# Last tile's gate logits from unnormalised rows, a seven-way threshold search, other counts of spare products, an earlier gather and a halved last group

## The chip, the cores and the metric

The kernel runs on one core of one Trainium2 chip. The metric is the device time in microseconds (us) of one execution. Three runs of the kernel before gave a median of 479.52 us (479.47 to 480.42). A core has five engines that run their own instruction streams and wait for one another on semaphores: TensorE (PE, matmuls), VectorE (DVE), ScalarE (ACT), GpSimd (POOL) and SyncE (SP, which here only issues DMAs).

## What is computed

The inputs are `x` (1250 rows of 512 features), 20000 edges, and weights. The reference, cut to what matters:

```python
xn = layernorm(x)
x = x + gnn(xn, edges, W1, b1, W2, b2) + mix(xn, Wq, Wk, Wv, mW1, mW2)   # two graph layers; linear attention
y = layernorm(x)                                  # 1250 rows, the "final" normalised rows
# routing, one group of 1250 tokens, 8 experts, m = 1250 // 8 = 156 places for each expert
logits = y @ gate_weight                          # 1250 x 8
t = log(clip(logits, 1e-6))
for _ in range(8):                                # Sinkhorn
    t = t - logsumexp(t, over tokens)
    t = t - logsumexp(t, over experts)
gates = exp(t)
vals, idx = top_k(gates.T, m)                     # the 156 best tokens of each expert
out = y[idx[e]] @ experts[e] * vals[e]            # for each expert e
x = x + scatter(out)                              # where two experts took a token, the later one stands
```

## The kernel before

The 1250 rows are ten tiles of 125. The kernel computes x's normalisation and K (to about 45 us), the attention terms, the adjacency counts and the first graph layer, then the second layer's aggregation tile by tile (from about 322 us), and then the routing and the experts.

At the start, SP issues the loads in an order written out by hand: x part 0, two chunks of Wk, x part 1, the other two chunks of Wk, the rest of x (L475 to L482). PE runs 12 spare products on a filled tile, transposes tile 0 (`turn_x(0)`, L714), runs 8 more spare products (`warm(WARMER)`, L715) and then the K products, in which the transposes of the next tiles stand at a fixed place (L718 to L722).

The stage around the change begins in the loop at L957. For tile i, `collect(i)` sums the aggregation in PSUM (L930 to L950). DVE (loop at L1727) adds it to X, takes mean and variance, waits for ACT's reciprocal root (L1265), makes the final factor in three small steps (`inverse_root`, L1306 to L1308) and writes the normalised row Y (L1737). PE transposes Y (`turn_y`, L913), ACT copies the transposes (`copy_yt`, L1250), and PE multiplies by the gate weights (`logits`, L920). For the last tiles PE runs 8 spare products (`keep_clock`, L952) while it waits; they write a PSUM bank that nobody reads. SP stores X and Y of each tile to a scratch tensor in HBM (`store_x`, `store_y`) and then loads the other experts.

Next come eight Sinkhorn rounds on P8 (125 x 10 x 8): DVE sums over the tiles, PE sums over the partitions by a product with ones (L974), DVE takes the reciprocal and scales, then normalises over the experts (L1751 to L1757). Each round has 4 spare products on PE behind the sum. Then ten rounds of a search for each expert's threshold, three bits of the number's pattern at a time (L1759 to L1772). DVE compares P8 with 8 candidates for each expert in two halves of five tiles (MASK), PE counts by ten products with ones (L983) and runs 4 spare products, and DVE keeps the largest candidate that at least 156 tokens reach (MET, kth) and makes the next candidates (THR).

From the threshold DVE and PE compute ties, ranks and each token's slot (L1783 to L1817), and one product gives the token number of each of the 128 slots in ten columns: eight experts, and two groups that hold 32 places for each of four experts beyond their 128 (`slots`, L1000 to L1005). DVE turns it into indices (L1827 to L1829), after which GpSimd gathers rows of scratch (`gather`, L620). The gate values go through a like product (`gates`, L1008), with 7 spare products before and 11 behind it. Each column is then transposed (`turn_slot`), copied (L1277, L1281), multiplied by its expert (`expert`, L1021) or, for the two groups, by four experts in strips of 32 (`rests`, L1035), weighed and added by DVE (`weigh`, L1848) and scattered to the output by GpSimd (L630). The order of the columns is one group, the eight experts, the other group.

The order on every engine is written out in the program. PSUM banks are given out by `psum_plan` (L71), which names who must have read a bank before it is opened again. `link` (L1288) makes DVE wait for its own last instruction; without it the next one may start before the last has written.

## Time and profile before

| what | value |
|---|---|
| median of three runs | 479.52 us |
| the profiled execution | 480.92 us |
| its span | 479.2 us |
| mean granted clock of PE | 0.983 |
| busy: PE, PE weight loads, DVE, ACT, POOL | 96%, 77%, 68%, 30%, 12% |
| the chain that ended last | PE 88%, DVE 7%, DMA 2% |

The profile is one execution, and its times count from the span's start. The chain of waits is followed back from the last instruction, at each step to what released it. The granted clock is given as a share of PE's full 2.4 GHz. Ends of matmuls are modelled, so a matmul's own duration is longer than its distance to the next; distances between starts are the better measure. The stages stand at these times: K products to 45 us, graph and attention products to 322 us, the aggregation tiles to 377.9 us, Sinkhorn from 383.9 us, the search from 400.8 us, ranks and slots from 425.2 us, gather and experts from 433 us to the end.

### The profile page before, as it was taken

How to read it: one execution, taken by the hardware profiler on the slowest of the kernel's cores; microseconds unless marked ns; L12 is line 12 of the kernel's file. 1: busy time of each engine (PE TensorE's matmuls, PEld its weight loads, DVE VectorE, ACT ScalarE, POOL GpSimd, SP SyncE). 2: the span in 40 equal slices, each digit the busy share in tenths (PEclk: the TensorE clock that was granted, in tenths of full speed). 3: DMA queues.
4: the chain of work that ended last, by engine and by line, in shares of the span. 5: the costliest groups of instructions: out<-in, count | busy, mean ns of one | idle time of the engine just before them, and what ended most of it. 6: DMA issues, size and time to landing. Idle time of an engine off the chain costs nothing.

```text
span 479.2 us, 6735 instructions
## 1 busy us (share of the span) xinstructions
PE 458.1 (96%) x2420; PEld 368.8 (77%) x2420; DVE 323.8 (68%) x1099; ACT 141.8 (30%) x244; POOL 57.7 (12%) x80
## 2 busy tenths in 40 slices
PE   7999999999999999999999999999999978877995
PEld 3787788888888888887789998778888855654782
DVE  6995698998998988896740112444446566676971
ACT  4676463333233232351231011221221135000120
POOL 4088100000000000000003000010000000005542
PEclk9999999999999999999999999999999987899998
DMA  7902004720000000003000000008444494005791
GB/s 221 271 1 88 2 0 122 182 89 23 0 2 0 2 0 1 2 1 124 1 1 3 1 0 3 0 0 288 149 130 130 131 359 166 1 1 198 262 346 76
DMA packets 20299, 40.43 MB, mean 84 GB/s; under 512 B 2408, under 2 KB 2738, under 8 KB 20259
## 3 DMA queue, kind: packets, MB, share of 16 engines
q1 hardware_dynamic: 18019, 32.53, 21.8%
q0 software_dynamic: 2240, 7.39, 4.2%
q8 instruction: 23, 0.38, 0.3%
q14 instruction: 17, 0.14, 0.1%
HBM read 30.09 MB, written 10.30 MB: 84 GB/s over the span
## 4 chain that ended last, share of the span: by engine, by line
PE 88%; DVE 7%; DMA 2%; issue 1%; SPq 0%; POOLq 0%; ACT 0%; DVEq 0%
PE ps L673 47%; PE ps L938 9%; PE ps L890 9%; PE ps L781 6%; PE ps L660 5%; PE ps L983 2%; PE ps L955 2%; PE ps L1044 2%; PE ps L923 1%; PE ps L1018 1%; DMA YX<-scratch,idx 1%; PE ps L813 1%; DMA X<-in_x 1%; PE ps L707 1%; PE ps L917 1%
## 5 line engine op out<-in xcount | busy, mean ns | idle before, releaser
L1554 DVE TENSOR_SCALAR RING_D<-places,PLACES 125x170 bf16<-125x170 f16 (+1 forms) x239 | 61.7, 258 | 0.0
L1555 DVE TENSOR_SCALAR RING_S<-iota,HOME 125x128 bf16<-125x128 f16 x239 | 58.5, 245 | 0.0
L890 PE MATMUL ps<-AT,H1H 125*128 125x416 f32 (+1 forms) x108 | 38.0, 352 | 0.0
L890 PE MATMUL ps<-AT,H1L 125*128 125x416 f32 (+1 forms) x108 | 38.0, 351 | 0.0
L938 PE MATMUL ps<-H2H,AT 125*125 125x512 f32 x90 | 36.2, 402 | 0.0
L938 PE MATMUL ps<-H2L,AT 125*125 125x512 f32 x90 | 35.5, 394 | 0.0
L955 PE MATMUL ps<-WE0H 128*128 128x512 f32 x109 | 35.3, 457 | 0.0
L1622 DVE TENSOR_TENSOR ps<-ps,bias 125x512 f32<-125x512 f32 x20 | 14.0, 699 | 27.9 <-PE ps L673 27.9
L1701 DVE SCALAR_TENSOR_TENSOR ZL<-ps,ZH 128x416 fp32r<-128x416 f32 (+1 forms) x12 | 6.3, 584 | 38.7 <-ACT ZH L1245 38.7
L660 PEld LDWEIGHTS ps<-RING_D,RING_S 125*125 125x125 bf16 x239 | 25.7, 136 | 7.9
L660 PE MATMUL ps<-RING_D,RING_S 125*125 125x170 bf16 (+1 forms) x239 | 28.6, 236 | 0.0
L565 POOL TENSOR_TENSOR G2L<-RAW_G,G2H 128x512 fp32r<-128x512 f32 x4 | 5.0, 1298 | 191.7 <-ACT G2H L1062 191.7
L621 POOL DMA_INDIRECT YX<-scratch,idx x10 | 11.9, 1188 | 112.3 <-DVE idx L1829 109.5
L955 PEld LDWEIGHTS ps<-WE0H 128*128 128x128 f32 x109 | 21.7, 218 | 3.3
L1195 ACT ACTIVATE AT<-ps 125x510 fp32r<-125x510 f32 (+1 forms) x25 | 14.8, 591 | 30.6 <-PE ps L660 30.6
L1730 DVE SCALAR_TENSOR_TENSOR X<-ps,X 125x512 f32<-125x512 f32 x10 | 6.9, 692 | 22.1 <-PE ps L950 22.1
L890 PEld LDWEIGHTS ps<-AT,H1H 125*128 125x128 f32 x108 | 20.3, 188 | 0.3
L890 PEld LDWEIGHTS ps<-AT,H1L 125*128 125x128 f32 x108 | 20.3, 188 | 0.2
L938 PEld LDWEIGHTS ps<-H2H,AT 125*125 125x125 f32 x90 | 16.7, 186 | 3.9
L938 PEld LDWEIGHTS ps<-H2L,AT 125*125 125x125 f32 x90 | 16.7, 186 | 3.8
L673 PE MATMUL ps<-CPH,QTH 128*125 128x512 f32 x40 | 17.4, 435 | 0.0
L673 PE MATMUL ps<-WQH,XTH 128*125 128x512 f32 x40 | 17.4, 435 | 0.0
(366 smaller groups left out, 1177.6 us busy)
## 6 DMA issues: line engine op xcount, KB each, us to landing
RAW_E<-in_experts SPq DMA_DIRECT2D x8, 1024.0 KB, 10.1
RAW_AGAIN<-in_experts SPq DMA_DIRECT2D x3, 1024.0 KB, 11.1
X<-in_x SPq DMA_DIRECT2D x1, 2240.0 KB
out_x<-X SPq DMA_DIRECT2D x10, 224.0 KB
scratch<-X SPq DMA_DIRECT2D x10, 224.0 KB
scratch<-Y SPq DMA_DIRECT2D x10, 224.0 KB
RAW_K<-in_WkT SPq DMA_DIRECT2D x4, 256.0 KB, 4.6
RAW<-in_mW2T SPq DMA_DIRECT2D x1, 1024.0 KB, 12.3
```

What stands on the lines that cost most here:

```text
L621: nc.gpsimd.indirect_dma_start(out=YX[0:SLOT, j % RING].rearrange("p a f -> p (a f)"), out_offset=None, in_=scratch, in_offset=bass.Indire ...
L660: pe.matmul(PS[4 + g % 2][0:TT, o:o + width(b)], hot_s(v)[:, 0:TT], hot_d(v, width(b)), start=(s == 0), stop=(s == VISITS[b] - 1), skip_gr ...
L673: mm = pe.matmul(ps, stationary[a](c), moving[b](c), start=(first and n == 0), stop=(last and n == len(pairs) - 1))
L781: mm = pe.matmul(ps[:], x[0:TT, i, f], e[0:TT, i % 4, :], start=(i == 0 and n == 0), stop=(i == NT - 1 and n == 2))
L890: pe.matmul(place(f), h[0:TT, k, 128 * f:128 * (f + 1)], AT[0:TT, k, c0:c1], start=(k == 0 and n == 0), stop=False)
L938: pe.matmul(ps, AT[0:TT, k, t], h[0:TT, k, :], start=(k == 0 and n == 0), stop=False)
L955: pe.matmul(PS[bank][:], WEH[0][:, 0, 0:128], WEH[0][:, 0, :], start=True, stop=True)
L983: mm = pe.matmul(ps[0:TT, 0:NE * WAYS], ones16[0:TT, 0:TT], MASK[0:TT, i].rearrange("p e c -> p (e c)"), start=(i == 0), stop=(i == NT - 1))
L1195: nc.scalar.activation(AT[0:TT, :, lo:hi], counts_of(g), ACT.Copy).then_inc(done["adj_hi"], 1)
L1554: V.tensor_scalar(hot_d(v, width(b)), places[0:ET, 0:width(b)], PLACES[0:ET, c:c + 1], None, ALU.is_equal)
L1555: V.tensor_scalar(hot_s(v), iota[0:ET, :], HOME[0:ET, c:c + 1], None, ALU.is_equal).then_inc(done["marked"], 1)
L1622: V.tensor_tensor(ps, ps, bias[layer - 1][0:TT, :], ALU.add).then_inc(done["h1_biased" if layer == 1 else "h2_biased"], 1)
```

## The change

1. The last tile's logits are computed from X, not from Y: `logits = rstd * (X @ gw) - mean * rstd * colsum(gw)`. PE transposes X(9) as soon as it is final (`turn_last`). The column sums of the gate weights come from a second load (`gw1`, behind x part 1) and four products with ones at the start, in the place of four of the eight spare products there. ACT copies the transposes of tiles 8 and 9 before it takes the last tile's root. Y(9) is written inside the first Sinkhorn round. The 8 spare products before the last tiles become 3 behind the last logits. The tables of the search and the two splits of expert 1 move to earlier tiles.
2. The search compares with seven candidates (the eighth, the threshold so far, is always reached and is copied into MET) and its masks are cut at tiles 6 and 4.
3. Six spare products follow each Sinkhorn sum (eight the last) where there were four.
4. DVE makes the indices ahead of the gate terms, and GpSimd's gathers wait for the first of the three index steps (`from_ready`). Two membership steps change places and one `link` goes.
5. The groups' transposed rows are copied in halves, and the last group's products and weighing run in two halves of its columns, the second in its own bank (`foot`).

The diff, cut to its core (declarations, semaphores' names and PSUM plan entries are left out):

```diff
 WAYS = 2 ** RADIX
+LANES = WAYS - 1
 HALF = NT // 2
+MASKED = [(0, 6), (6, NT)]
 TP = NE_T // 2
...
     load_x(1)
+    sp.dma_start(gw1[:], rows(gate_w[0])).then_inc(loads["gate1"], 16)
     load_wk(2)
...
     pool.wait_ge(done["st_scratch"], 2 * 16 * len(CUTS) * NT)
-    pool.wait_ge(done["idx_ready"], 1)
+    pool.wait_ge(done["from_ready"], 1)
...
     turn_x(0)
-    warm(WARMER)
+    pe.wait_ge(loads["gate1"], 16)
+    ps = opens("gsums")
+    for c in range(C):
+        mm = pe.matmul(ps[0:TT, 0:NE], ones[:, 0:TT], gw1[:, c, :], start=(c == 0), stop=(c == C - 1))
+    closes("gsums", mm)
+    warm(WARMER - 4)
     for i in range(NT):
...
+    def turn_last():
+        i = NT - 1
+        pe.wait_ge(done["x_final"], NT)
+        opens(f"yt{i}")
+        for c in range(C):
+            mm = pe.transpose(view(f"yt{i}")[:, c, 0:TT], X[0:TT, i, 128 * c:128 * (c + 1)], ident[0:TT, 0:TT])
+        closes(f"yt{i}", mm)
...
         pe.wait_ge(done["yt_ready"], i + 1)
+        ps = opens("last")[0:TT, 0:NE] if i == NT - 1 else PS[plan["logits"][0]][0:TT, NE * i:NE * (i + 1)]
         for c in range(C):
-            mm = pe.matmul(PS[plan["logits"][0]][0:TT, NE * i:NE * (i + 1)], YT[:, i % 2, c, 0:TT], gw[:, c, :],
-                           start=(c == 0), stop=(c == C - 1))
+            mm = pe.matmul(ps, YT[:, i % 2, c, 0:TT], gw[:, c, :], start=(c == 0), stop=(c == C - 1))
         if i == NT - 1:
+            closes("last", mm)
+        elif i == NT - 2:
             closes("logits", mm)
...
-    for i in range(NT + 2):
-        if i < NT:
-            collect(i)
-        if i == NT:
-            pe.wait_ge(done["x_final"], NT - 2)
-            pe.wait_ge(done["exp_hi"], 1)
-            keep_clock(8, plan[f"o{NT - 3}"][0])
-        if 1 <= i <= NT:
+    for i in range(NT):
+        collect(i)
+        if i:
             turn_y(i - 1)
...
             logits(i - 2)
+    turn_last()
+    logits(NT - 2)
+    logits(NT - 1)
+    pe.wait_ge(done["exp_hi"], 1)
+    keep_clock(3, plan[f"o{NT - 3}"][0])
...
                                      start=True, stop=True))
-        keep_clock(4, plan["order"][0])
+        keep_clock(6 if r + 1 < SINKHORN else 8, plan["order"][0])
     pe.wait_ge(done["rconsts"], 1)
...
         ps = opens(f"rad{r}")
-        for h in range(2):
+        for h, (lo, hi) in enumerate(MASKED):
             pe.wait_ge(done["ind_ready"], 2 * r + h + 1)
-            for i in range(HALF * h, HALF * (h + 1)):
-                mm = pe.matmul(ps[0:TT, 0:NE * WAYS], ones16[0:TT, 0:TT], MASK[0:TT, i].rearrange("p e c -> p (e c)"),
+            for i in range(lo, hi):
+                mm = pe.matmul(ps[0:TT, 0:NE * LANES], ones16[0:TT, 0:TT], MASK[0:TT, i].rearrange("p e c -> p (e c)"),
                                start=(i == 0), stop=(i == NT - 1))
...
-        pe.wait_ge(done["ftr_ready"], NC - COLUMNS[j])
-        ps = opens(f"fo{j}")
-        for c in range(C):
-            if c == 2 and between is not None:
-                between()
-            for q in range(4):
-                p = slice(REST * q, REST * (q + 1))
-                mm = pe.matmul(ps[p, :], FTR[:, c, p], raw[q][:, c, :], start=(c == 0), stop=(c == C - 1), skip_group_check=True)
-                if c == C - 1:
-                    mm.then_inc(done["rest_ready"], 1)
-        closes(f"fo{j}", pe.nop())
+        pe.wait_ge(done["ftr_half"], NC - COLUMNS[j])
+        parts = [(f"fo{j}", 0, D)] if between is not None else [(f"fo{j}", 0, D // 2), ("foot", D // 2, D)]
+        for name, lo, hi in parts:
+            ps = opens(name)
+            for c in range(C):
+                if c == 2:
+                    pe.wait_ge(done["ftr_ready"], NC - COLUMNS[j])
+                    if between is not None:
+                        between()
+                for q in range(4):
+                    p = slice(REST * q, REST * (q + 1))
+                    mm = pe.matmul(ps[p, 0:hi - lo], FTR[:, c, p], raw[q][:, c, lo:hi], start=(c == 0), stop=(c == C - 1),
+                                   skip_group_check=True)
+                    if c == C - 1:
+                        mm.then_inc(done["rest_ready"], 1)
+            closes(name, pe.nop())
...
             split_expert(i - 4)
+        if i == NT - 1:
+            copy_yt(i - 1)
+            copy_yt(i)
         if i < NT:
...
                                  bias=eps[0:TT, 0:1]).then_inc(done["sqrt2_ready"], 1)
-        if i:
+        if 0 < i < NT - 1:
             copy_yt(i - 1)
...
                 act.wait_ge(done["rest_ready"], 4)
-            copy(FTR[:], view(f"ft{j}")).then_inc(done["ftr_ready"], 1)
+            copy(FTR[:, 0:2], view(f"ft{j}")[:, 0:2]).then_inc(done["ftr_half"], 1)
+            copy(FTR[:, 2:C], view(f"ft{j}")[:, 2:C]).then_inc(done["ftr_ready"], 1)
         else:
...
     split_lo("wk", 3)
+    reads(dve, "gsums")
+    V.tensor_copy(gate_sum[t], ps_of("gsums")[t, 0:NE]).then_inc(done["gsum_ready"], 1)
     moments(2, statistics(2))
...
+    def normal_row(i):
+        V.tensor_scalar(Y[0:TT, i, :], X[0:TT, i, :], mv[0:TT, i, 0:1], rstd[0:TT, 2, i:i + 1],
+                        ALU.subtract, ALU.mult).then_inc(done["y_ready"], 1)
+    def radix_tables():
+        after("rconsts", 1)
+        for r, s in enumerate(SHIFTS):
+            V.tensor_scalar(ctab[:, r, :], lane[:], WAYS - 1, s, ALU.bitwise_and, ALU.logical_shift_left)
+        V.tensor_scalar(THR[:], lane[:].unsqueeze(1).broadcast_to([128, NE, LANES]), WAYS - 1, SHIFTS[0], ALU.bitwise_and,
+                        ALU.logical_shift_left)
+        V.memset(MET[:, :, 0:1], 0.0)
...
         after("inv2_ready", i + 1)
-        V.tensor_scalar(Y[0:TT, i, :], X[0:TT, i, :], mv[0:TT, i, 0:1], rstd[0:TT, 2, i:i + 1],
-                        ALU.subtract, ALU.mult).then_inc(done["y_ready"], 1)
-        if i in (6, 7):
-            expert_left(1, i - 6)
-    after("rconsts", 1)
-    for r, s in enumerate(SHIFTS):
-        V.tensor_scalar(ctab[:, r, :], lane[:], WAYS - 1, s, ALU.bitwise_and, ALU.logical_shift_left)
-    V.tensor_scalar(THR[:], lane[:].unsqueeze(1).broadcast_to([128, NE, WAYS]), WAYS - 1, SHIFTS[0], ALU.bitwise_and,
-                    ALU.logical_shift_left)
+        if i < NT - 1:
+            normal_row(i)
+        if i in (5, 6):
+            expert_left(1, i - 5)
+        if i == 7:
+            radix_tables()
+    i = NT - 1
+    link(V.scalar_tensor_tensor(away[t, i:i + 1], mv[t, i, 0:1], -1.0, rstd[t, 2, i:i + 1], ALU.mult, ALU.mult))
+    link(V.tensor_scalar(last8[t, 0, :], gate_sum[t], away[t, i:i + 1], None, ALU.mult))
     reads(dve, "logits")
-    link(V.tensor_scalar(P8[t], ps_of("logits")[t, 0:NT * NE].rearrange("p (i e) -> p i e", e=NE), CLIP_EPS, None, ALU.max))
+    V.tensor_scalar(P8[t, 0:i, :], ps_of("logits")[t, 0:i * NE].rearrange("p (i e) -> p i e", e=NE), CLIP_EPS, None, ALU.max)
+    reads(dve, "last")
+    link(V.scalar_tensor_tensor(last8[t, 1, :], ps_of("last")[t, 0:NE], rstd[t, 2, i:i + 1], last8[t, 0, :], ALU.mult, ALU.add))
+    link(V.tensor_scalar(P8[t, i, :], last8[t, 1, :], CLIP_EPS, None, ALU.max))
     for r in range(SINKHORN):
...
+        if r == 0:
+            normal_row(NT - 1)
         reads(dve, f"sink{r}")
...
     for r in range(len(SHIFTS)):
-        for h in range(2):
-            w = slice(HALF * h, HALF * (h + 1))
-            V.tensor_tensor(MASK[t, w], P8[t, w].unsqueeze(3).broadcast_to([TT, HALF, NE, WAYS]),
-                            THR[t].bitcast(F32).unsqueeze(1).broadcast_to([TT, HALF, NE, WAYS]),
-                            ALU.is_ge).then_inc(done["ind_ready"], 1)
+        for lo, hi in MASKED:
+            shape = [TT, hi - lo, NE, LANES]
+            V.tensor_tensor(MASK[t, lo:hi], P8[t, lo:hi].unsqueeze(3).broadcast_to(shape),
+                            THR[t].bitcast(F32).unsqueeze(1).broadcast_to(shape), ALU.is_ge).then_inc(done["ind_ready"], 1)
+        if r:
+            V.tensor_copy(MET[t, :, 0], kth[t])
         reads(dve, f"rad{r}")
-        V.scalar_tensor_tensor(MET[t], ps_of(f"rad{r}")[t, 0:NE * WAYS].rearrange("p (e c) -> p e c", c=WAYS), float(TOPK),
-                               THR[t].bitcast(F32), ALU.is_ge, ALU.mult).then_inc(done["count_read"], 1)
+        V.scalar_tensor_tensor(MET[t, :, 1:WAYS], ps_of(f"rad{r}")[t, 0:NE * LANES].rearrange("p (e c) -> p e c", c=LANES),
+                               float(TOPK), THR[t].bitcast(F32), ALU.is_ge, ALU.mult).then_inc(done["count_read"], 1)
         after("count_read", r + 1)
...
         if r + 1 < len(SHIFTS):
-            link(V.tensor_tensor(THR[t], kth[t].bitcast(I32).unsqueeze(2).broadcast_to([TT, NE, WAYS]),
-                                 ctab[t, r + 1, :].unsqueeze(1).broadcast_to([TT, NE, WAYS]), ALU.bitwise_or))
+            link(V.tensor_tensor(THR[t], kth[t].bitcast(I32).unsqueeze(2).broadcast_to([TT, NE, LANES]),
+                                 ctab[t, r + 1, :].unsqueeze(1).broadcast_to([TT, NE, LANES]), ALU.bitwise_or))
...
     running(ahead, mine).then_inc(done["order_in"], 1)
-    V.tensor_scalar(member[t, 0, :], top[t], GROUPS * 2 + 0.5, None, ALU.is_lt)
+    V.tensor_scalar(member[t, 1, :], top[t], GROUPS * 2 + 0.5, None, ALU.is_gt)
     V.tensor_scalar(shift32[t, 0, :], top[t], float(REST), -float(REST + SLOT), ALU.mult, ALU.add)
-    link(V.tensor_scalar(member[t, 1, :], top[t], GROUPS * 2 + 0.5, None, ALU.is_gt))
+    link(V.tensor_scalar(member[t, 0, :], top[t], GROUPS * 2 + 0.5, None, ALU.is_lt))
+    V.scalar_tensor_tensor(shift32[t, 1, :], member[t, 1, :], -4.0 * REST, shift32[t, 0, :], ALU.mult, ALU.add)
...
-    link(V.scalar_tensor_tensor(shift32[t, 1, :], member[t, 1, :], -4.0 * REST, shift32[t, 0, :], ALU.mult, ALU.add))
     reads(dve, "order")
...
+    reads(dve, "slots")
+    u = slice(0, SLOT)
+    ps = ps_of("slots")[u, 0:NC]
+    V.tensor_scalar(idx[u, 0, :], ps, -1.0, 0.0, ALU.add, ALU.max).then_inc(done["from_ready"], 1)
+    link(V.tensor_scalar(tokv[u, 2, :], ps, 0.0, 8192.0, ALU.is_equal, ALU.mult))
+    V.scalar_tensor_tensor(idx[u, 1, :], ps, -1.0, tokv[u, 2, :], ALU.add, ALU.add).then_inc(done["idx_ready"], 1)
     V.tensor_scalar(side[t, 0, :], rank[t, 0, :], full_slots, None, ALU.is_lt)
...
     link(V.tensor_reduce(gres[t, 0, :], w8[t].rearrange("p e i -> p i e"), AX, ALU.add))
-    reads(dve, "slots")
-    u = slice(0, SLOT)
-    ps = ps_of("slots")[u, 0:NC]
-    V.tensor_scalar(idx[u, 0, :], ps, -1.0, 0.0, ALU.add, ALU.max)
-    link(V.tensor_scalar(tokv[u, 2, :], ps, 0.0, 8192.0, ALU.is_equal, ALU.mult))
-    V.scalar_tensor_tensor(idx[u, 1, :], ps, -1.0, tokv[u, 2, :], ALU.add, ALU.add).then_inc(done["idx_ready"], 1)
...
             dve.wait_ge(scattered[j % 4], 16 * (j // 4))
-        V.scalar_tensor_tensor(FO[u, j % 4, :], ps_of(f"fo{j}")[u, :], tokv[u, 1, column(j)], YX[u, j % RING, 1, :],
-                               ALU.mult, ALU.add).then_inc(done["fo_ready"], 1)
+        for name, lo, hi in ([(f"fo{j}", 0, D)] if j + 1 < NC else [(f"fo{j}", 0, D // 2), ("foot", D // 2, D)]):
+            if lo:
+                reads(dve, name)
+                after("rest_ready", 12)
+            ins = V.scalar_tensor_tensor(FO[u, j % 4, lo:hi], ps_of(name)[u, 0:hi - lo], tokv[u, 1, column(j)],
+                                         YX[u, j % RING, 1, lo:hi], ALU.mult, ALU.add)
+        ins.then_inc(done["fo_ready"], 1)
```

## Rows read from the trace of the kernel before

**Rows 1.** The page: granted clock in 40 slices; the chain by engine.

```profile
PEclk9999999999999999999999999999999987899998
...
PE 88%; DVE 7%; DMA 2%; issue 1%; SPq 0%; POOLq 0%; ACT 0%; DVEq 0%
```

**Rows 2.** Waits of PE, 30 to 60 us: us in total, times, longest.

```profile
PE ps L726 <- DVE diag L1492: 0.3, 1, 0.3
```

**Rows 3.** Stretches: busy time of each engine, then PEclk, DMA share, GB/s.

```profile
384.00:386.00 2.00, 1.72 (x6) 1.38 (x6) 1.36 (x6) 0.00 (x0) 0.00 (x0) 0.63 0.90 294
...
402.00:404.00 2.00, 2.00 (x10) 1.53 (x9) 1.27 (x5) 1.60 (x1) 0.00 (x0) 0.50 0.00 0
```

**Rows 4.** Timeline of the last tile: start us, us, engine, line, operation, idle before.

```profile
377.47 0.39 PE L950 MATMUL ps<-H2L,AT 125*125 125x512 f32 x1
...
379.57 0.29 ACT L1265 ACTIVATE rstd<-mv,eps 125x1 f32<-125x1 f32 x1 [5.15 <-DVE mv L1733]
...
379.77 0.57 ACT L1062 ACTIVATE YT<-ps 128x500 f32<-128x500 f32 x1
...
380.65 0.55 DVE L1737 TENSOR_SCALAR Y<-X,mv,rstd 125x512 f32<-125x512 f32 x1
...
381.73 1.88 PE L923 MATMUL ps<-gw,YT 128*125 128x8 f32 x16
...
383.93 0.29 DVE L1751 TENSOR_REDUCE s<-P 125x8 f32<-125x80 f32 x1
```

**Rows 5.** Timeline of the start, 6.8 to 12 us.

```profile
6.86 1.85 PE L696 MATMUL ps<-HOT_D 128*128 128x500 bf16 x8
...
7.36 0.69 DVE L1322 BATCH_NORM_STATS2 stat<-X 125x6 f32<-125x512 f32 x1 [0.50 <-DMA X<-in_x]
...
9.49 1.40 DVE L1340 TENSOR_SCALAR XF<-X,mv,rstd 125x512 f32<-125x512 f32 x1
...
9.78 0.63 ACT L1062 ACTIVATE WKH<-RAW_K 128x512 fp32r<-128x512 f32 x1 [0.53 <-DMA RAW_K<-in_WkT]
...
10.95 0.65 PE L707 MATMUL ps<-ident,XF 125*128 125x125 f32 x4 [0.86 <-DVE XF L1340]
```

**Rows 6.** DMA issues of the whole span: KB, us from issue to landing.

```profile
gw<-in_gate SPq DMA_DIRECT2D x1, 16.0 KB, 2.0
```

**Rows 7.** Timeline of one Sinkhorn round.

```profile
390.98 1.18 PE L955 MATMUL ps<-WE0H 128*128 128x512 f32 x4
...
392.82 0.38 PE L974 MATMUL ps<-s,ones 125*125 125x8 f32 x2 [0.66 <-DVE s L1751]
```

**Rows 8.** The chain in order of time, search: start us, us, what.

```profile
402.58 1.87 PE ps L955 x4
...
405.46 1.87 PE ps L955 x4
...
414.26 0.50 DVE MASK L1762
...
416.50 0.50 DVE MASK L1762
```

**Rows 9.** Timeline behind the search, 431 to 440 us.

```profile
431.72 0.30 PE L1004 MATMUL ps<-PLACE,RS 125*128 125x10 f16 x5 [0.36 <-DVE RS L1817]
...
432.70 0.17 DVE L1829 SCALAR_TENSOR_TENSOR idx<-ps,tokv 128x10 int32<-128x10 f32 x1
...
435.04 2.79 PE L955 MATMUL ps<-WE0H 128*128 128x512 f32 x11
...
438.34 0.66 PE L1018 MATMUL ps<-ident,YX 128*128 128x128 f32 x4 [0.52 <-DMA YX<-scratch,idx]
...
439.03 0.60 ACT L1062 ACTIVATE FTR<-ps 128x512 f32<-128x512 f32 x1 [34.72 <-PE ps L1018]
```

**Rows 10.** The chain in order of time, last group.

```profile
470.40 3.69 PE ps L1044 x32
...
474.17 0.76 DVE FO L1856
```

24 lines of the change are left out of this document (15 added, 9 removed).

## The prediction

> **What bounds the kernel now.** I read the page first, then the chain of waits, then the stretches by clock. The page gives 88% of the chain to TensorE (PE) and 7% to VectorE (DVE) [rows 1]. From 12 us to 377.8 us the waits show PE waiting for another engine once, for 0.3 us [rows 2], so whatever delays it early is carried to the end and nothing there takes it back. From 377.8 us on the work is serial: DVE and PE hand small results to each other, and each instruction's latency counts. The second row of the page's picture shows something more: the granted clock is below 9 tenths in three slices, all in this serial part [rows 1]. In the table of stretches the clock goes to its lower level, 1.2 of 2.4 GHz (0.50), after 384.5 us, and again from 401.6 to 411.8 us [rows 3]. The first follows a stretch in which PE had only transposes and gate products of 8 columns (381.25 to 383.6 us) and waited [rows 4]; the second follows the last Sinkhorn round with its four spare products and the wait for the first mask.
>
> **The start.** A second load of the gate weights (512 pieces of 32 bytes) goes into SyncE's queue behind the second x part and ahead of the last two chunks of Wk and all further x. Four column-sum products (8 instructions, 0.87 us at the rate of the gate products, 16 in 1.88 us [rows 4], of which about 1.74 to the next start) take the place of four spare products of 8 that took 1.85 us [rows 5]: 0.87 for 0.9, nothing. But PE now waits for the load. On an idle queue the same load landed in 2.0 us [rows 6]. Here it stands behind x, whose landing DVE awaited until 7.36 us [rows 5], so I put it at about 7.9 to 8.4 us, against the 7.0 us at which PE is free. That moves the first K product from 8.9 to 9.8 or 10.2 us. PE stood idle for 0.86 us ahead of the transposes of the second tile [rows 5], and that idle time takes 0.86 of it. The other path is the Wk chunk: ScalarE (ACT) already waited 0.53 us for the last one [rows 5], so each tenth that the load takes from the DMA engines arrives there, less some 0.4 us of slack before DVE takes it up at 10.81 us, and one copy of the sums (0.17) joins DVE's queue. Ends: nothing, if the load lands with x, to +1.6, if PE's wait brings the clock down as it did at 384.5 us, so that four spare and four K products run at half rate (8 times 0.21). I take +0.7, between, nearest to the path by Wk. A GpSimd subtraction ran beside DVE's normalising of tile 1, which took 1.40 us [rows 5], where the same step on the last Y took 0.55 [rows 4]. A later Wk chunk may part the two, and then 0.85 us of the loss comes back. The Trainium skill says so too (SBUF — State Buffer, on the port pair that VectorE and GpSimd share, an exclusive lock: whoever comes second blocks); by that rule alone the start costs nothing, and the total would be 0.7 us lower.
>
> **The last tile.** Before, the way from the last aggregation product to the first column sum of the Sinkhorn part is 377.88 to 383.93 us: residual, statistics, root, three small steps, Y, transposes, copy, products, clip [rows 4]. After, the transposes of X run beside the statistics and the products beside the root, so that DVE's chain is last. It is longer than it looks, since ACT must finish the copy of tile 9's transposes before the root: transposes from 378.95 to about 379.55 us, copy 0.57 [rows 4], root at 380.18 instead of 379.57, so 0.61 late. Then the three steps as before (0.78 to their signal: 381.26), and in place of Y five operations: away and last8 at 0.25 each with their waits, the clip of nine tiles at 0.15 since nothing waits for it, the joining and the last clip at 0.25 each. The column sum starts at 382.41, 1.52 us earlier. PE's products end near 381.3 us and are not late. Y of the last tile (0.55) moves beside the first column-sum product; that reply took 0.46, so 0.1 is not covered. Sum: -1.4. The store of Y is 2 us later on SyncE, and the loads of experts 2 to 7 behind it too; the last of these was split at 404.3 us and is needed after 450 us. The tables of the search move to tile 7, into DVE idle time of over 1.2 us per tile. Were neither covered, 2 us and 1 us would be at stake.
>
> **Sinkhorn with six spare products.** A round is 2.08 us at full clock. PE's share is 0.38 plus four products at 0.21, and it then idles 0.66 us by the modelled ends [rows 7]; two more take 0.43, so they are hidden at full clock, and so are the eight of the last round. At half clock four took 1.87 [rows 8], 0.47 each: six and the sum product take 3.2 us, 1.1 us more than a round. The kernel before lost 0.2 to its half-clock stretch here. Ahead of this part the change takes eight spare products away and puts three back, with gate products and a wait around them, so that PE has even less to do from 377.8 us on and I expect the clock to fall once here too. One round and a bit at 3.2 costs 1.1; against the 0.2 of before, +0.9. Ends: -0.2 (no fall) and +2 (two rounds).
>
> **The search.** At half clock its round was 2.88 us (402.58 to 405.46), at full clock 2.24 (414.26 to 416.50) [rows 8], and ten rounds took from 400.82 to 425.18 us, where ten full ones less the last threshold update take 22.1: 2.2 us lost. PE set the pace in them: its ten products and four spare ones left no gap. Eight spare products at the end of Sinkhorn, where four had preceded the fall, should keep the clock: -2.2 (0 if they don't). Seven lanes for eight and the cut at 6 and 4 tiles save 80 of 640 elements, 0.08 us, on the second mask only; the first grows by 16 elements, 0.02 us, and the ten products follow it without a gap, bound by their weight loads (0.80 us for ten). The added copy of kth runs during DVE's wait of 0.57. So the lanes come to 0, at most 0.1 a round either way.
>
> **Behind the search.** Reordering the membership steps takes one wait off the path: -0.1. The gather waits for the first index only, and the indices now stand ahead of the gate terms. The product for the slots ends at 432.02 us, the first index would start at 432.06 and be ready at 432.25, where 432.87 was the third's end [rows 9]: the first gather is 0.63 earlier, and lands at 437.7 for 438.34. But the gate terms are pushed back by 0.5 (three index steps now stand ahead), and PE's eleven spare products with them: issued from 435.04, they end by 437.4 [rows 9], now 437.9. PE so takes up the gathered rows at 437.9: -0.45, not -0.63. Copying the transposed rows in halves lets the group start after half of 0.60 [rows 9]: -0.25. Sum: -0.7. The gate terms' half microsecond also delays DVE's splits, which had 2.84 us free before the first expert. **The last group** in column halves: before, 3.69 us of products, then 0.76 on DVE [rows 10]. Half the columns take DVE about 0.48, so -0.3 if the products take no longer. There are 64 for 32, each half as long; four that go to different strips start together every 0.43 us, and in the search weight load and product pairs were 56 ns apart, which for 4 pairs is 0.22, as long as 256 columns last. Ends: -0.35 and +0.3. The Trainium skill (TensorE: Matmul & The Clock Gate, "Wait — 56ns, not 53.3ns?") has about 62 ns per MATMUL of sequencer time in one of the two ways of decoding. By it, 64 products would take 4.0 us and the step would win nothing; the pairs at 56 ns of this trace speak for the other way, not strongly.
>
> **The sum.** +0.7 - 1.4 + 0.9 - 2.2 - 0.1 - 0.7 - 0.3 = -3.1. The profiled execution took 480.92 us, 1.7 more than its span, so the sum gives 477.8. The median of the three runs is 1.40 below that execution. If the whole of it is overhead of profiling, the median after is 476.4. If the runs behind the median had no half-clock stretch in the search, 2.2 of the gain is not theirs and they come to 478.6. I take 477.5.
>
> **Rivals.** (1) The clock stays up from the last tile to the end, as it did from 412 us on [rows 1]; then the Sinkhorn term is -0.2 and the start costs 0 to 0.7: 475.9 to 476.6, say 476.3. Against it: fewer spare products exactly where it fell. (2) The gain is paid back at half clock: the wait for the gate load brings the clock down at the start (+1.6) and Sinkhorn loses two rounds (+2): 479.5, within 0.2%. For it: the start's spare work is halved and stands behind a DMA. (3) The spare products don't do what they are for, and the search runs at half clock as before: 477.5 + 2.2 = 479.7. This is weakened by the fact that four per round kept the clock from 412 us on. (4) Slower: six spare products are too many at half clock. Once down, PE is the pace of Sinkhorn, 3.2 for 2.08 us; if the fall is not taken back after one round, each further round adds 1.1, and all eight add 8, to about 485. It decides from four rounds on (477.5 + 3.3 = 480.8). Against it: the clock came back at 387.9 us after a stretch in which PE was busy throughout at half rate, and six products make it busier.
>
> **Chances.** Forecast 0.52, rival (1) 0.22, (2) 0.12, (3) 0.10, (4) 0.04. A difference under 0.2% (0.96 us) cannot be told from none here. Faster by over that is 478.56 or less: the forecast and (1), and a quarter of (2) and (3), 0.78 together. Within it 0.18, slower 0.04. The range reaches from below rival (1) to the edge of (2): 475.4 to 479.5.
>
> **What would show it.** First column sum at about 1.5 us after the three small steps, and 4.5 us, not 6.05, behind the last product; root about 0.6 late behind the copy. The search's rounds all 2.24 us with a granted clock of 1.00; Sinkhorn rounds of 3.2 us under 0.50. Transposes of the first gathered rows right behind the last of eleven spare products, with no wait for the DMA. DVE's last operation near 0.48 us. The first K product at about 10 us. I am wrong if the search still has rounds of 2.88 us, or if the first K product starts after 11 us.

## The result, and the profile after

The changed kernel takes 477.36 us in the median of five runs (476.29 to 477.96); in the same rounds the kernel before took 479.55 us (479.47 to 480.88). The ratio on record is 0.9928, with a 95% interval from 0.9908 to 0.9947: faster by 0.5 to 0.9%. It isn't the quotient of these two medians, which is 0.9954; it fits the 480.5 to 480.8 us that the kernel before took beside the experiments. A second set of runs of the unedited changed kernel (experiment 10) gave 476.88 against 480.75 us, a ratio of 0.9925. The forecast was 477.5 us.

The two profiled executions are 477.36 us (span 475.3) and 480.92 us (span 479.2). This is the page of after, its granted clock in 40 slices and its chain by engine, to be held against [rows 1]:

```profile
PEclk9999999999999999999999999999999979999999
...
PE 89%; DVE 7%; issue 1%; DMA 1%; SPq 0%; POOLq 0%; ACT 0%; DVEq 0%
```

Four slices were below 9 before, three in the serial part and the last one, which lies behind the last product; one is now. The table cuts both executions at the same DVE instructions. X(9) is the start of the last residual, "sum" the first column sum of Sinkhorn, "mask" the first mask of the search, RS the first of the two instructions that write RS.

| stretch, us | before | after | forecast | measured |
|---|---|---|---|---|
| start of the span to X(9) | 377.90 | 378.13 | +0.7 | +0.2 |
| X(9) to sum | 6.03 | 4.29 | -1.5 | -1.7 |
| sum to mask (Sinkhorn) | 16.89 | 18.16 | +1.0 | +1.3 |
| mask to the ties (search) | 24.36 | 21.61 | -2.2 | -2.75 |
| ties to RS (ranks) | 4.94 | 4.82 | -0.1 | -0.1 |
| RS to the first expert's FTL | 12.94 | 12.42 | -0.7 | -0.5 |
| FTL to the end of the last FO | 31.86 | 31.63 | -0.3 | -0.2 |
| span | 479.2 | 475.3 | -3.1 | -3.9 |

(The forecast's -1.4 for the last tile is here its two parts, -1.5 and the 0.1 that Y costs inside the first round.)

The timeline of after around the last tile: start us, us, engine, line, operation, idle before. It answers [rows 4].

```profile
378.13 0.69 DVE L1779 SCALAR_TENSOR_TENSOR X<-ps,X 125x512 f32<-125x512 f32 x1 [2.63 <-PE ps L974]
...
379.15 0.62 PE L939 MATMUL ps<-ident,X 125*128 125x125 f32 x4
...
379.61 2.18 PE L946 MATMUL ps<-gw,YT 128*125 128x8 f32 x16
...
379.81 0.59 ACT L1091 ACTIVATE YT<-ps 128x500 f32<-128x500 f32 x1 [0.66 <-PE ps L939]
...
380.30 0.28 ACT L1297 ACTIVATE rstd<-mv,eps 125x1 f32<-125x1 f32 x1
...
381.97 0.22 DVE L1799 SCALAR_TENSOR_TENSOR last<-ps,rstd,last 125x8 f32<-125x8 f32 x1
...
382.42 0.30 DVE L1803 TENSOR_REDUCE s<-P 125x8 f32<-125x80 f32 x1
382.64 0.54 DVE L1764 TENSOR_SCALAR Y<-X,mv,rstd 125x512 f32<-125x512 f32 x1
...
386.06 0.42 PE L998 MATMUL ps<-s,ones 125*125 125x8 f32 x2
...
386.34 2.34 PE L979 MATMUL ps<-WE0H 128*128 128x512 f32 x6
386.52 0.21 DVE L1807 RECIPROCAL s<-ps 125x8 f32<-125x8 f32 x1 [1.37 <-PE ps L998]
```

The way from X(9) is DVE's chain with ACT's root in it: the root stands behind the copy on ACT and starts at 380.30 us, as the copy's record ends (380.40). PE's products for the last logits are done when L1799 wants them, since no wait stands behind it. Y lies beside PE's first column-sum product. At 386 us each column sum waits for six spare products at half rate: DVE stands for 1.37 us. The stretches of after, busy time of each engine, then PEclk, DMA share, GB/s, show where the clock went:

```profile
379.00:381.00 2.00, 2.00 (x20) 2.00 (x20) 1.08 (x4) 0.91 (x3) 0.00 (x0) 1.00 0.63 192
381.00:383.00 2.00, 2.00 (x8) 1.68 (x8) 1.79 (x9) 0.00 (x0) 0.00 (x0) 0.51 0.18 65
...
402.00:404.00 2.00, 1.55 (x14) 1.07 (x14) 1.56 (x6) 1.91 (x1) 0.00 (x0) 1.00 0.25 95
```

By the trace's record of the granted clock, from which all such times below are, it is at 1.2 GHz (0.50) from 381.0 to 387.9 us, behind a stretch in which PE had only transposes and gate products of 8 columns. From then to 473 us, behind the last product, it stays at 2.4 GHz; the stretch that stood at 0.50 in [rows 3] for 402 to 404 us is gone. The chain in order of time, one round of the search (against [rows 8]), and the last group (against [rows 10]):

```profile
402.77 0.52 DVE MASK L1816
...
403.43 0.75 PE ps L1007 x10
...
404.96 0.52 DVE MASK L1816
...
466.77 3.71 PE ps L1072 x64
...
470.58 0.50 DVE FO L1915
```

A round is 2.19 us, all alike. The 64 half-wide products take 3.71 us where 32 took 3.69, and DVE's last operation 0.50 for 0.76. Behind the search, timeline of after (against [rows 9]):

```profile
430.02 1.18 POOL L630 DMA_INDIRECT YX<-scratch,idx  x1 [105.58 <-DVE idx L1878]
...
432.37 2.78 PE L979 MATMUL ps<-WE0H 128*128 128x512 f32 x11
...
434.98 0.60 PE L1042 MATMUL ps<-ident,YX 128*128 128x128 f32 x4
...
436.25 1.92 PE L1072 MATMUL ps<-RAW_E,FTR 128*32 128x512 f32 x16 [0.67 <-ACT FTR L1091]
```

The transposes stand right behind the eleven spare products and no longer wait for the gather. The start, timeline of after (against [rows 5]):

```profile
7.71 0.69 DVE L1355 BATCH_NORM_STATS2 stat<-X 125x6 f32<-125x512 f32 x1 [0.69 <-DMA X<-in_x]
...
7.94 1.04 PE L727 MATMUL ps<-gw,ones 128*125 128x8 f32 x8 [0.76 <-DMA gw<-in_gate]
...
9.50 0.58 PE L682 MATMUL ps<-WKH,XTH 128*125 128x512 f32 x1
...
9.54 1.29 POOL L574 TENSOR_TENSOR WKL<-RAW_K,WKH 128x512 fp32r<-128x512 f32 x1 [0.76 <-ACT WKH L1091]
...
9.71 0.63 ACT L1091 ACTIVATE WKH<-RAW_K 128x512 fp32r<-128x512 f32 x1 [0.24 <-DMA RAW_K<-in_WkT]
...
9.84 1.28 DVE L1373 TENSOR_SCALAR XF<-X,mv,rstd 125x512 f32<-125x512 f32 x1
...
11.18 0.65 PE L716 MATMUL ps<-ident,XF 125*128 125x125 f32 x4 [0.40 <-DVE XF L1373]
```

### The profile page after: what moved, and what is told of

Its sections match the earlier page's. It is cut to its first block, busy times and chain, and to the rows that moved or that the text cites. A ratio compares the mean times of both kernels' runs of the same rounds, so it can differ in the third digit from the quotient of the medians.

```text
span 475.3 us, 6855 instructions
## 1 busy us (share of the span) xinstructions
PE 457.3 (96%) x2469; PEld 370.8 (78%) x2469; DVE 324.4 (68%) x1115; ACT 141.6 (30%) x246; POOL 57.6 (12%) x80
## 4 chain that ended last, share of the span: by engine, by line
PE 89%; DVE 7%; issue 1%; DMA 1%; SPq 0%; POOLq 0%; ACT 0%; DVEq 0%
PE ps L682 47%; PE ps L962 9%; PE ps L904 9%; PE ps L795 6%; PE ps L669 5%; PE ps L979 2%; PE ps L946 2%; PE ps L1007 2%; PE ps L1072 2%; DVE MASK L1816 1%; DMA X<-in_x 1%; PE ps L1042 1%; PE ps L827 1%; PE ps L716 1%; PE ps L931 1%
## 5 line engine op out<-in xcount | busy, mean ns | idle before, releaser
L1589 DVE TENSOR_SCALAR RING_D<-places,PLACES 125x170 bf16<-125x170 f16 (+1 forms) x239 | 63.3, 265 | 0.0
L1590 DVE TENSOR_SCALAR RING_S<-iota,HOME 125x128 bf16<-125x128 f16 x239 | 60.2, 252 | 0.0
L979 PE MATMUL ps<-WE0H 128*128 128x512 f32 x122 | 36.5, 434 | 0.0
L979 PEld LDWEIGHTS ps<-WE0H 128*128 128x128 f32 x122 | 23.1, 205 | 3.7
L682 PE MATMUL ps<-MPH,XTH 128*125 128x512 f32 x40 | 17.4, 436 | 0.0
```

The source lines that it names most:

```text
L682: mm = pe.matmul(ps, stationary[a](c), moving[b](c), start=(first and n == 0), stop=(last and n == len(pairs) - 1))
L979: pe.matmul(PS[bank][:], WEH[0][:, 0, 0:128], WEH[0][:, 0, :], start=True, stop=True)
L1589: V.tensor_scalar(hot_d(v, width(b)), places[0:ET, 0:width(b)], PLACES[0:ET, c:c + 1], None, ALU.is_equal)
L1590: V.tensor_scalar(hot_s(v), iota[0:ET, :], HOME[0:ET, c:c + 1], None, ALU.is_equal).then_inc(done["marked"], 1)
```

## The experiments

Every kernel was timed in five rounds against the kernel before on its own chip, which took 480.51 us (18 runs) beside the first four, 480.69 us (17) beside the next four and 480.75 us (17) beside the last four. Stage times are from one profile each, and what a half-clock stretch costs differs from one execution to the next. The changed kernel itself was timed only in the first comparison and on the chip of the last four, so the other medians are compared with it by their ratios.

**1. Four spare products in Sinkhorn again.** The changed kernel with

```diff
-                keep_clock(6 if r + 1 < SINKHORN else 8, plan["order"][0])
+                keep_clock(4, plan["order"][0])
```

> The changed kernel with four spare products behind every Sinkhorn sum, the eight of the last round included, as before the change. Theory A (six and eight keep the clock up into the search, but cost 1.1 us a round where the clock is down): Sinkhorn, 18.2 us in the changed kernel's profile from the first column sum to the first mask, is 16.9 to 17.3 us where the clock falls ahead of it; the search, 21.6 us, is the same if the clock stays up and up to 2.3 us longer where it falls at the end of Sinkhorn, so the runs spread more upward. Median within 0.7 us of the changed kernel's. Rival (the spare counts matter in neither place): both stages unchanged. Rival (the counts carry the whole gain): the search is at half clock in the profile and the median is over 2 us above the changed kernel's.

Median 476.8 us (476.0 to 480.29, 12 runs), ratio 0.9937 (0.9917 to 0.9956). A stretch of this kernel:

```profile
400.00:402.00 2.00, 1.58 (x12) 1.33 (x12) 0.85 (x4) 1.49 (x1) 0.00 (x0) 0.50 1.05 387
```

The clock is down from 381.9 to 392.1 us, and again from 398.9 to 405.8. A round at 0.50 is 2.30 us with four and 2.99 with six, so four cost 0.2 a round and six 0.9; but with four the first low stretch is longer, and the second comes back: the search takes 22.78 us instead of 21.61. The Sinkhorn stage is 17.55 us, above the 16.9 to 17.3 that theory A gave. Half of its twelve runs took 476.0 to 476.2 us, less than the changed kernel's median, and the others 477.4 to 480.3; the ratio can't be told from the changed kernel's 0.9928. The fall at the end of Sinkhorn is what four don't prevent.

**2. Four in the first two rounds, six in the others.** In the same line, `4 if r < 2 else 6 if r + 1 < SINKHORN else 8`.

> The changed kernel with four spare products in the first two Sinkhorn rounds, six in the next five, eight in the last. Theory A: where the clock is down in the first two rounds they take about 2.3 us instead of 2.4 and 3.0, so Sinkhorn takes about 17 us instead of 18.2 and the median is about 1 us below the changed kernel's (476.4), with the search at full clock. Rival: with less for PE to do, the clock stays down longer, over three or four rounds, and the loss is the same as with six (Sinkhorn 18 us or more).

Median 476.53 us (475.62 to 478.42, 6 runs), ratio 0.9925 (0.99 to 0.995). The rounds are 2.29, 2.29, 2.30, 2.98 us; the clock is down from 381.5 to 391.8 us. The Sinkhorn stage is 18.33 us, not shorter than after's 18.16. In this profile the clock stays down longer than in after, so nothing is won. That four products were the reason is not shown: with six, the same first fall lasted 6.8 us in four profiles and 3.4 us in two (experiments 3 and 8).

**3. Eight lanes and the cut at five tiles again.** `LANES = WAYS`, `MASKED = [(0, HALF), (HALF, NT)]`, MET written whole and no copy of kth.

> The changed kernel with the search as before: eight candidates, the masks cut at tiles 5 and 5, no copy of kth. Theory A (seven lanes and the cut at 6 and 4 gave the 0.05 us a round that the traces show, 2.235 to 2.185, because the ten products end 0.05 us sooner): a round takes 2.235 us again at full clock, the search 22.1 us instead of 21.6, and the median rises by 0.5 us. Rival (the prediction's: lanes and cut are worth nothing): rounds of 2.185 us stay.

Median 477.9 us (477.07 to 478.43, 7 runs), ratio 0.9947 (0.9925 to 0.9969). The chain of this kernel, one round:

```profile
402.02 0.50 DVE MASK L1816
...
402.66 0.80 PE ps L1007 x10
...
404.25 0.50 DVE MASK L1816
```

A round is 2.23 us, and the search 22.08 us against 21.61: lanes and cut are worth 0.05 us a round and 0.5 us in all. The ten products go from 0.80 to 0.75 us, but not because they have 56 columns for 64. The first five of one round, in this kernel and then in after:

```profile
418.29 0.45 PE L1007 MATMUL ps<-MASK,ones 125*125 125x64 bf16 x5 [0.44 <-DVE MASK L1816]
```

```profile
418.72 0.45 PE L1007 MATMUL ps<-MASK,ones 125*125 125x56 bf16 x5 [0.43 <-DVE MASK L1816]
```

Five take 0.45 us at either width. Single products start 0.058 us apart in both kernels, except that with the cut at five tiles the sixth starts 0.085 us behind the fifth and the seventh 0.079 behind the sixth, since PE reaches the second half before DVE has its mask ready. With the cut at six and four tiles the second mask is shorter and comes in time (both masks take 0.81 us for 0.89), and the 0.05 us of waiting are gone. The longer first mask costs 0.02, and 56 elements for 64 in DVE's small steps give 0.02 back.

**4. The gate load behind the third chunk of Wk.** The load and `load_wk(2)` change places, the column sums move into the first K products, and all eight spare products stay ahead.

> The changed kernel with the gate load one place later in SyncE's queue (behind the third Wk chunk), all eight spare products at the start, and the column-sum products inside the first K product, just ahead of the transposes of tile 1, where PE waits. Theory A (the start costs 0.23 us because the load delays x part 1, which DVE takes up at 7.71 us instead of 7.36, and PE's own wait is covered): DVE takes x part 1 up at about 7.4 us, the transposes of tile 1 begin at 10.95 to 11.0 us, and the last aggregation product ends 0.2 us earlier than in the changed kernel (378.13), at 377.9. Rival (the prediction's: the cost comes by the Wk chunks and DVE's queue): the transposes begin at 11.1 us or later and the end of aggregation stays at 378.1 or moves up. The median moves by 0.2 us at most, less than can be told.

Median 476.56 us (475.67 to 477.32, 6 runs), ratio 0.9922 (0.99 to 0.9943). DVE takes up the second part of x at 7.70 us (after: 7.71), and tile 1 is transposed at 11.16 us (11.18): the later place brings nothing. In three profiles of the old start X(9) begins at 377.58, 377.90 and 377.99 us, in ten of the changed start between 377.54 and 378.59, mean 378.11, and here at 378.14. The start is dearer by about 0.3 us in the mean, which is less than it scatters from one execution to the next.

**5. The spare products spread around the last tile.**

```diff
+            pe.wait_ge(done["exp_hi"], 1)
+            keep_clock(1, plan[f"o{NT - 3}"][0])
             turn_last()
             logits(NT - 2)
+            keep_clock(1, plan[f"o{NT - 3}"][0])
             logits(NT - 1)
-            pe.wait_ge(done["exp_hi"], 1)
-            keep_clock(3, plan[f"o{NT - 3}"][0])
+            keep_clock(5, plan[f"o{NT - 3}"][0])
```

> The changed kernel with seven spare products around the last tile's logits where it has three: one ahead of the transposes of X, one between the last two tiles' gate products, five behind them. Theory A (the clock falls in this part because PE has hardly any long product from 378 us to 383 us, and the fall costs 0.6 to 1.7 us in the first Sinkhorn rounds): the clock stays at 1.00 into the Sinkhorn part or falls in fewer executions, Sinkhorn takes 16.7 us in the profile instead of 17.3 to 18.4, the first column sum comes 0.1 to 0.3 us later because of the product that stands ahead of the last gate products, and the median is about 1 us under the changed kernel's. Rival (transposes and gate products count as little as before and seven are too few): the fall stays, and since five spare products at half clock take 2.1 us, the stage gets 0.5 to 1 us longer.

Median 475.87 us (475.71 to 477.17, 6 runs), ratio 0.9911 (0.9892 to 0.9931). Timeline of this kernel, then its stretches:

```profile
379.20 0.48 PE L979 MATMUL ps<-WE0H 128*128 128x512 f32 x1
...
380.73 0.48 PE L979 MATMUL ps<-WE0H 128*128 128x512 f32 x1
```

```profile
381.00:383.00 2.00, 2.00 (x14) 1.63 (x13) 1.76 (x10) 0.00 (x0) 0.00 (x0) 1.00 0.24 81
```

The clock stays at 1.00 from the start's rise to 471.2 us, behind the last product. The first product delays the last transposes and with them copy and root (root 2.45 us behind X(9), 0.28 later than in after), so X(9) to sum is 4.58 us for 4.29; against that Sinkhorn takes 16.69 us for 18.16, rounds 2.08 to 2.10. The fall stood behind the last tile in all eight profiles with the changed order there and stays away in all three with this one (experiments 5, 9 and 12), so it comes from what PE has to do around the last tile. Two of the six runs took 477.1 and 477.2 us at a mean granted clock of 0.995 and 0.994, where the others had 0.997 to 0.999; what they lost is not seen in a profile. In after it came at 381.0 us, before PE reached the first of the three spare products behind the logits (381.65 us); more of them there alone could not have stopped it. Which of the two products ahead is needed, and whether five behind are, was not separated.

**6. The root ahead of the copy, and nine spare products behind the gate values.** `copy_yt(i)` of the last tile goes behind the ACT root, and `keep_clock(11, ...)` becomes 9.

> The changed kernel with two edits in separate stages. (1) ACT takes the last tile's root ahead of the copy of its transposes. Theory A (the prediction's chain: DVE is last by little, PE's gate products end only about 0.1 us before DVE takes them up): the root comes 0.5 us earlier, the copy and the products 0.2 us later, and the stage from residual to first column sum stays at 4.3 us, PE being last. Rival: PE had slack, and the stage falls to 3.8 us. (2) Nine spare products behind the gates' products, where it has eleven. Theory A (PE's spare products hold the transposes of the first gathered rows back, by up to 0.4 us): the stretch from the last slot mask to the first FTL falls from 12.42 to about 12.1 us. Rival (the rows land no earlier than PE is free): 12.4 us stays. The clock stays at 1.00 there in both.

Median 476.06 us (475.72 to 477.03, 5 runs), ratio 0.9904 (0.9886 to 0.9923). Timeline of this kernel:

```profile
379.66 0.29 ACT L1296 ACTIVATE rstd<-mv,eps 125x1 f32<-125x1 f32 x1 [0.65 <-DVE mv L1783]
379.86 0.57 ACT L1091 ACTIVATE YT<-ps 128x500 f32<-128x500 f32 x1
...
381.90 0.23 DVE L1800 SCALAR_TENSOR_TENSOR last<-ps,rstd,last 125x8 f32<-125x8 f32 x1 [0.47 <-PE ps L946]
...
434.59 0.66 PE L1042 MATMUL ps<-ident,YX 128*128 128x128 f32 x4
```

The root is 0.50 us earlier in relation to X(9), and the stage takes 4.37 us instead of 4.29: DVE arrives early and waits 0.47 us for PE's last gate products, which the later copy holds back. The two paths are level, so the order of the change is as good. Nine spare products for eleven take RS to FTL from 12.42 to 12.05 us: PE's spare work had indeed become the last thing there.

**7. The kernel before with six spare products (eight in the last round) and nothing else.**

> The kernel before, with six spare products behind each Sinkhorn sum and eight behind the last, and nothing else. Theory A (the spare products are the part of the change that keeps the search at full clock; four per round let it fall in some executions, at a cost of 1 to 2.3 us): the search takes 22.1 us in the profile, and the median is 0.5 to 1.2 us under that of the kernel before, with the upper runs gone. Where the clock falls ahead of Sinkhorn, each round there costs up to 0.9 us more than before. Rival (a coincidence of the two profiles): the search has a half-clock stretch here too, and the median is that of the kernel before or above.

Median 478.98 us (478.5 to 481.51, 12 runs), ratio 0.9974 (0.996 to 0.9988). A stretch of this kernel:

```profile
402.00:404.00 2.00, 1.55 (x14) 1.07 (x12) 1.56 (x5) 1.59 (x1) 0.00 (x0) 1.00 0.00 0
```

The search takes 22.08 us and Sinkhorn 16.70, with the clock at 1.00 throughout. By the ratio this part alone is worth 0.26% of 480.7, 1.2 us, of the change. The upper runs are gone but for one: eleven of the twelve lie between 478.5 and 479.8 us, and one took 481.51. The fall in the first Sinkhorn rounds is absent too, so six spare products with the old order around the last tile had no fall at all ahead of the kernel's end in this profile. That points to the changed order there as what brings the fall of the changed kernel; it is one profile.

**8. The late index, and the last group whole.** The index steps go back behind the gate terms, GpSimd waits for the last of them, and the last group's products and weighing are whole again; the halved copies of FTR stay.

> The changed kernel with the indices behind the gate terms and the gather waiting for all three steps, as before, and with the last group in one piece; the transposed rows are still copied in halves. Theory A: the stretch from the last slot mask to the first FTL is 12.7 us instead of 12.42, 0.3 longer (PE's spare products now end 0.5 us earlier, but the rows land 0.6 later), and the last operation of DVE takes 0.75 instead of 0.48, so that the stretch from the first FTL to the end of the last FO is 31.86 instead of 31.62. Together +0.5 in the profile, too little for the median to tell well. Rival (the halving of FTR alone gives the 0.5 of the first stretch): 12.42 stays.

Median 477.46 us (476.85 to 477.96, 6 runs), ratio 0.9937 (0.9919 to 0.9955). Timeline of this kernel:

```profile
430.21 1.18 POOL L630 DMA_INDIRECT YX<-scratch,idx  x1 [105.30 <-DVE idx L1884]
...
434.81 0.66 PE L1042 MATMUL ps<-ident,YX 128*128 128x128 f32 x4 [0.54 <-DMA YX<-scratch,idx]
```

RS starts at 426.56 us here and at 427.01 in after. The gather is issued 3.65 us behind it (after 3.01), the transposes start 8.25 us behind it (after 7.97) and wait for the DMA again; RS to FTL is 12.76 us for 12.42, and FTL to the end 31.84 for 31.63. So the index order is worth 0.3 us and the halved last group 0.2.

**9. Experiment 5's spreading with nine spare products behind the gate values.**

> The changed kernel with both edits that gained alone: the spare products spread around the last tile (one before the last transposes, one between the last two logits, five behind them) and nine instead of eleven behind the gate products. Theory A: they lie in different stages and add up. Clock at 1.00 from the last tile to the experts, first mask about 16.7 us behind the first column sum, first group's weighing about 12.05 us behind RS; median 475.5 (475.2 to 475.9), 1.6 below the changed kernel run on the same chip. Theory B: the saved 0.37 us behind the gate products is taken by PE standing idle there, and the clock falls among the experts: a stretch at 0.50 after 435 us and a median near 476.5 or above.

Median 475.65 us (475.52 to 477.55, 5 runs), ratio 0.9903 (0.9882 to 0.9924): 1.2 us below the unedited changed kernel on the same chip (experiment 10). The clock stays at 1.00 until behind the last product. The timeline:

```profile
431.33 2.31 PE L979 MATMUL ps<-WE0H 128*128 128x512 f32 x9
433.51 0.42 PEld L1044 LDWEIGHTS ps<-ident,YX 128*128 128x128 f32 x4 [0.29 <-DMA YX<-scratch,idx]
433.52 0.66 PE L1044 MATMUL ps<-ident,YX 128*128 128x128 f32 x4
```

The two gains add up: X(9) to sum 4.58, Sinkhorn 16.71, RS to FTL 12.04 us. The transposes come 7.54 us behind RS (425.98). Their first weight load stands idle for 0.29 us until the gather has landed (issued at 428.99 us, landed 4.5 us later), and in experiment 6 it is the same with 0.30. With nine products PE and the gather are level, so fewer than nine would win nothing. It is the fastest kernel of the study; its slowest run took 477.55 us.

**10 and 11. Both kernels, unedited, profiled a second time.**

> The changed kernel with nothing edited, as the yardstick on the same chip as the others of this call. Theory A: the fall of the clock in the first Sinkhorn rounds is a property of the code (what PE has to do there), so it comes again: one stretch at 0.50 that begins between 380.5 and 384 us, Sinkhorn stage 17.2 to 18.4 us, search 21.6 us at 1.00, median 476.5 to 477.5. Theory B: it was that one execution's chance; then no stretch, Sinkhorn 16.7 us and a profiled span near 474.

> The kernel before with nothing edited, profiled a second time. Theory A: its second stretch at half clock, in the search, comes in nearly every execution, since four spare products a round leave PE too little to do at the end of Sinkhorn: 0.50 begins between 398 and 403 us again, and the search takes 23.5 to 25 us. Theory B: it comes in some executions only, and the median (1.4 us below the profiled execution) is of those without it: then the search takes 22.1 us in this profile, whose device time is then near 478.7.

The changed kernel: median 476.88 us (476.48 to 478.46, 6 runs), ratio 0.9925 (0.9907 to 0.9944). The kernel before: 480.09 us (478.94 to 482.11, 12 runs), ratio to the other runs of the same kernel 0.999 (0.9972 to 1.0007). Stretches, first of the changed kernel, then of the kernel before:

```profile
381.00:383.00 2.00, 2.00 (x7) 1.64 (x8) 1.58 (x7) 0.00 (x0) 0.00 (x0) 0.50 0.01 5
```

```profile
387.00:389.00 2.00, 2.00 (x7) 1.31 (x6) 1.18 (x6) 1.07 (x1) 0.00 (x0) 0.50 1.03 392
...
402.00:404.00 2.00, 2.00 (x12) 1.35 (x12) 1.50 (x5) 1.82 (x1) 0.00 (x0) 0.61 0.00 0
```

The changed kernel repeats itself: clock down from 380.5 to 387.3 us, 4.30, 18.14, 21.60 us for the three stages. The kernel before has both its falls again, but of other lengths: from 385.4 to 392.2 us and from 402.5 to 405.9 us. The search takes 22.55 us, not 24.36, which neither expectation gave: the fall came both times, and what it cost was 0.5 us once and 2.2 us the other time. The spans of this second pair of profiles, 477.8 and 474.7 us, are 3.1 us apart, those of the first pair 3.9.

**12. The spreading of experiment 5 with four spare products in every Sinkhorn round.**

> The changed kernel with the spare products spread around the last tile and four spare products in each of the eight Sinkhorn rounds, as before the change. Theory A: the two falls have separate causes, so the first stays away and the second comes: Sinkhorn rounds 2.08 us, a stretch at 0.50 that begins near 399 us and costs 1.0 to 2.3 us in the search (22.6 to 23.9 us instead of 21.6); median 476.5 to 478. Theory B: the second fall follows from the first (the clock that has just come back falls more easily), so with the first gone it stays at 1.00 with four too: search 21.6 us, median 475.9.

Median 476.29 us (476.24 to 476.8, 4 runs), ratio 0.9911 (0.9891 to 0.9931). A stretch of this kernel:

```profile
394.00:396.00 2.00, 2.00 (x6) 1.08 (x6) 1.44 (x6) 1.20 (x2) 0.00 (x0) 0.52 1.05 391
```

The clock falls at 394.1 us and is back at 397.5. Sinkhorn is 16.95 us and the search 21.61. So a fall with four products a round doesn't need the first one; here it comes inside Sinkhorn, where PE has slack, and so costs 0.25 us only. It hit neither expectation's time: the fall was foretold, its place and price weren't.

## Why the prediction was right, and where it was not

**The total** was right, 477.5 for 477.36 us, and the profiled spans differ by 3.9 us for a forecast 3.1. The ratio on record, 0.9928, is 3.5 us of 480; the two medians of the first comparison are only 2.2 us apart, which lies outside its interval. The second pair of profiles gives just 3.1 us, but only because the kernel before lost less at half clock in it (search 22.55 us for 24.36). By its terms the total should have come out lower: the start was 0.5 us cheaper than forecast, the search 0.5 us and the last tile 0.2 us better, against Sinkhorn 0.3 us dearer and the gather and the last group 0.3 us poorer. What brought the number near is the next step.

**From execution to median.** I had two readings of the 1.40 us between the profiled execution and the median: overhead, or no half-clock stretch in the median's runs. Neither holds. The runs of the kernel before beside the experiments, on three chips, go from 478.8 to 482.7 us, and in experiment 11's twelve the mean granted clock goes with them: 0.990 at 478.94 us, 0.983 at 480.97, 0.975 at 482.11. The same code loses different amounts of time at half clock each time, and the profiled 480.92 us (0.983) lies in the middle of these. The first comparison's median of before, 479.55 us, is of five runs and 1 us below the medians of 17 and 18 beside the experiments. That the forecast for the median hit within 0.2 us is therefore luck; the sum against the spans is the fairer test.

**The start** (+0.7, measured +0.2, and 0.3 in the mean of ten). The sums wait for the load as said (0.76 us, first K product at 9.50 us and not 10). The term was mis-sized on the side of Wk: ACT waited 0.24 us for the last chunk, not longer than the 0.53 of [rows 5], and experiment 4 moved the load with no effect. What sets the start is another operation. In 13 of the 14 profiles X(9) begins 366.95 to 367.00 us behind the transposes of tile 1, and these begin 0.34 us behind the end of GpSimd's subtraction of the third Wk chunk. It began at 9.33 us before and at 9.54 us after, which is 0.21 of the 0.23 us of the table. It holds XF back. The subtraction of before, then three rows of experiment 8's kernel, whose start is that of after:

```profile
9.33 1.28 POOL L565 TENSOR_TENSOR WKL<-RAW_K,WKH 128x512 fp32r<-128x512 f32 x1 [0.87 <-ACT WKH L1062]
```

```profile
9.76 0.55 DVE L1373 TENSOR_SCALAR XF<-X,mv,rstd 125x512 f32<-125x512 f32 x1
...
10.29 1.28 POOL L574 TENSOR_TENSOR WKL<-RAW_K,WKH 128x512 fp32r<-128x512 f32 x1 [1.50 <-ACT WKH L1091]
...
11.62 0.18 PEld L682 LDWEIGHTS ps<-WKH,XTH 128*125 128x125 f32 x1 [0.51 <-POOL WKL L574]
```

In the same 13 profiles the subtraction starts first, and XF, whenever it starts, ends 0.27 to 0.29 us behind its end and so takes 0.97 to 1.53 us. The Trainium skill (SBUF — State Buffer, "Who interferes with whom") has the later of the two fully blocked until the first is done, for a VectorE instruction of the kind that takes both ports. The rows of XF agree with that. In experiment 8's profile the third chunk came late and parted the two, as the prediction thought it might: XF took 0.55 us. Yet nothing came back, since the K products then waited for the late subtraction (0.51 us), and X(9) at 378.59 us is the latest of all.

**The last tile** (-1.5, measured -1.7: the stage took 4.29 or 4.30 us in all seven profiles with this order). The order was as said: copy, root 2.17 us behind X(9) where I had 2.28, three steps, five operations, PE not late. The five take 1.06 us (from 381.36 to 382.42 us) for my 1.15; the sign that asks for the column sum 1.5 us behind the three steps doesn't fit that working, which has 1.15. Experiment 6 shows the choice of ACT's order to be neutral, which I had not priced. Y in the first round costs 0.02 us and not 0.1 (first round of experiment 5 2.10 us, the others 2.08).

**Sinkhorn** (+1.0, measured +1.3). The mechanism was right, one fall behind the last tile, and experiment 5 shows its cause by taking it away. The price was off: not one round of 3.2 us but three of 2.43, 2.99 and 2.31, which is 1.5 us over 2.08; six spare products at 0.50 make a round of 2.99, since they start 0.43 us apart and not 0.47. This price too is one execution's. In the profiles of experiments 3 and 8, whose kernels are the same up to here, the clock was back after 3.4 us and not 6.8, and the stage took 17.31 and 17.24 us, only 0.4 more than before. The other end, -0.2, is where experiments 5 and 9 are (16.69 and 16.71 us for 16.89). Rival (1) was thus open to seven spare products around the last tile in place of three.

**The search** (-2.2, measured -2.75). The spare products do what the step said: in experiment 7 alone they take the search to 22.08 us with the clock at 1.00, as 22.1 was forecast. Rival (3) is out. But the -2.2 is the price of one execution's fall; experiment 11 has 0.5 us, and experiment 1 1.2 us with four products. The term for the lanes and the cut was mis-sized: I put it to 0 because the ten products would follow the first mask "without a gap", at the pace of their weight loads. The pace was right, 0.058 us a product at 64 and at 56 columns (the prediction's 56 ns is a little low). The gap was what it missed: in the old kernel PE waited 0.05 us for the second mask in each round, and the new cut takes that wait away (experiment 3). The round fell by 0.05 us, inside the bound of 0.1 that the text gave but worth 0.5 us in all.

**Behind the search.** The order of the membership steps: -0.1, as said. The gather: issued 0.64 us earlier (forecast 0.63), the gate products 0.44 us later (0.5), the transposes behind PE's spare products and not behind the DMA, all as said. Yet the transposes came 0.25 us earlier than before in relation to RS (7.97 us behind it for 8.22), not 0.45: from the start of the eleven spare products to that of the transposes it is 2.61 us, where I had taken 2.36. The mis-sized term is the spare products' time: 2.4 us is from the start of the first to the start of the last (435.04 and 437.44 us in before), and the transposes can follow only one product later. Before is also the low end here: in the three profiles with the old order behind the search the transposes stand 8.22, 8.49 and 8.33 us behind RS and FTL 12.94, 13.21 and 13.06, so that against their mean the stage gained 0.65 us, near the 0.7 of the forecast. The halved FTR: from the transposes to FTL 4.45 us for 4.72, -0.27 for -0.25.

**The last group** (-0.3, measured -0.2). The products take 3.71 us, so halving them is free, and DVE's operation gives 0.26. The Trainium skill (TensorE: Matmul & The Clock Gate, "Wait — 56ns, not 53.3ns?") has about 62 ns of sequencer time per MATMUL in one of its two decodings, by which 64 would take 4.0 us. The row of 64 in 3.71 us (58 ns each) doesn't bear it out here.

**Rivals (2) and (4).** Nothing was paid back at the start. In Sinkhorn the fall lasted some two and a half rounds in both profiles of the changed kernel, and cost 1.5 us; rival (4) wanted four rounds of 3.2 us.

**Small slips in the working.** The picture of [rows 1] has four slices below 9 and not three. Rival (1)'s own terms give 475.7 to 476.4 us, 0.2 under what the text has. A quarter of (2) and (3) is 0.055, which makes 0.795 and not 0.78. None of them moves the forecast or its range.

## What to carry to other kernels

Where the chain runs through short dependent steps, look at the granted clock first, and at what PE did before it fell. Here that was transposes and gate products of 8 columns, and a spare product in each of two gaps ahead of the fall paid (0.3 us of delay for 1.5 us saved, with five behind), where a row of three behind it came too late. Too many spare products cost little at full clock and 0.9 us a round once it has fallen, and each that stands in front of real work should be counted again when the wait it filled gets shorter, as with eleven that should have become nine; there the gather is the last to come again. A group of short products that is fed in two parts should be looked at start by start: one count for all ten hid a wait of 0.05 us between the parts. A stretch at half clock in one profile is a sample: profile the same kernel twice before its price goes into a sum.

## What the runs showed of the chip

- The same code falls to 1.2 GHz at the same place but for different times: the kernel before was down in the search from 401.6 to 411.8 us in one execution and from 402.5 to 405.9 us in the other, with an effect of 2.2 and 0.5 us on the stage.
- Products into four strips of 32 with 256 columns keep the pace of half of those with 512: 64 in 3.71 us, 32 in 3.69.
- bf16 products with ones, each with its own weight load of 125 columns, start 0.058 us apart at 56 and at 64 columns alike: narrower masks don't make them faster.
- A normalising step of VectorE (125x512, f32, 0.55 us alone) that starts behind a GpSimd subtraction (1.28 us) ended 0.27 to 0.29 us behind its end in all 13 profiles where the two met, wherever in it it started. GpSimd's subtraction took 1.28 to 1.30 us with the step beside it and 1.28 without (experiment 8).
- A second load of 16 KB in small pieces into the queue at the start, between x and Wk, can't be told from the scatter of the start, 377.5 to 378.6 us at X(9) in ten executions.
- Not settled: what differs between two executions that makes the same fall last from 3 to 10 us. The runs show that it varies, not why.
